# Gathering the first four edge groups straight from the node rows, a table in node order, and a short last group

## The chip, the cores and the metric

The kernel runs on one core of one Trainium2 chip. The metric is the device time of one execution in microseconds (us). The engines are named as in the profile: PE is TensorE (PEld its weight loads), DVE is VectorE, ACT is ScalarE, POOL is GpSimd, SP is SyncE; SPq, POOLq and ACTq are the queues on which these issue DMAs.

## The reference, cut to what matters

```python
x = x + conv(quantise(ln_c(x)), quantise(weight), bias)        # 16 x 64 x 56 x 56
t = tokens(x)                                                  # M = 50176 nodes of 64 channels
h = (ln(t) @ W_gat).reshape(M, 4, 4)                           # 16 features of a node
src, dst = edges + self loops                                  # 262144 edges
a_src, a_dst = (h * att_src).sum(-1), (h * att_dst).sum(-1)    # 4 heads
e = leaky_relu(a_src[src] + a_dst[dst], 0.2)
alpha = exp(e - segment_max(e)) / segment_sum(exp(...))
agg = segment_sum(h[src] * alpha, dst)
scores = layernorm(agg + b_gat).mean over heads                # 4 experts
t = t + sum over the top 2 experts of gate * (gelu(ln(t) @ W1 + b1) @ W2 + b2)
```

The factors exp(a_src - amax) and exp(0.2 (a_src - amax)) depend on the source node only, with amax the maximum over all nodes for each head. They are multiplied on an edge with a factor of its destination.

## The kernel before, in words

There are three stages. In the first, the edges are sorted into 49 blocks of 1024 destination nodes, while the pixels are normalised, quantised and convolved. Its first DVE operations (lines 720 to 733) split the edge list: line 722 takes the block of the destination, lines 725 to 727 turn the source number into a place `(node & 127) * 392 + (node >> 7)`, and lines 728 and 729 code that place in 16 bits. The stage leaves the sorted edges in DRAM (`edge_d`) and one row of 24 floats (96 B) for each node in `node_d`: 16 features, 4 values a_src, 4 values a_dst. The node rows are stored by line 370, two DMAs of 1568 rows for each image.

The second stage is the one that is changed. Edges come as 1090 units of 256 at most (`MAX_UNITS`); 8 units are a group, so there are NG = 137 groups of 16 tiles of 128 edges. The units behind the last real one are padding and read row 0. At the start of the stage:

- SP loads the sorted edges (line 1066), then all node rows into `nodes` with four DMAs (line 1070, 4704 KB in pieces of 96 B).
- DVE decodes the source numbers (line 1329 writes `src_no` and signals `src_ready`), makes the first one-hot masks, waits for the nodes, finds amax (lines 1351 to 1356) and the gaps (lines 1358 to 1360).
- ACT makes `damp` and overwrites the last 8 columns of `nodes` with the two factors (lines 1103 to 1106, `factors_ready`).
- SP then stores the whole table to `tab_d` with one DMA (line 1073), in an order in which each partition writes one contiguous piece (392 rows, 37632 B), and behind it, on the same queue, loads the first tokens `T` (line 1076).
- POOL waits for `src_ready` and `table_stored` (lines 1090 and 1091) and issues one indirect DMA for each tile: 128 rows of 96 B by the numbers in `src_no` (line 1097). `gath` has 4 buffers (`BUFS`) of one group; from group 4 on POOL waits for `rows_used`, which DVE raises in `weigh`.

For each group g, DVE waits for the 16 gathers and weighs the rows (`weigh`, lines 1384 to 1386), spreads them (line 1394, `spread_ready`), and adds up the sums of the group (`add_up`, line 1406) as PE delivers them. PE goes through a fixed order (`body`, line 1255): `up` of the MLP (line 1243, waits for `t_loaded`), half of `scatter` (line 1234, waits for `spread_ready`), transposes of the masks of group g+2 (line 1210), `down` (line 1253), the other half of `scatter`, and `pick_dst` for group g+2 (line 1220, 16 matmuls of 32 columns in two halves). The MLP is part of the bodies of groups 0 to 127; groups 128 to 136 have none. ACT does gelu (line 1120), the bias of the second layer (line 1129), the copies of the turned masks (line 1115) and of the destination factors (line 1142), in an order written out by hand. The first bodies of ACT and PE are unrolled; DVE runs a loop over 33 trips of 4 groups and 5 more groups.

Then the sums are divided and normalised, the gates are made, and the third stage adds the gated experts. Nothing of that is touched.

Of the kernel before, what the change touches and what calls it, by code (L numbers as in the profile page):

```python
# [10 lines left out]
U16 = mybir.dt.uint16  # L11
# [4 lines left out]
P = 128  # L16
# [69 lines left out]
TILES = NG * G  # L86
ID_W = -(-NG * UG // P)
# [52 lines left out]
def build(nc, x, conv_w, conv_b, w_gat, att_src, att_dst, b_gat, ln_g, ln_b, w1, b1, w2, b2, edges, out):  # L140
    ctx = ExitStack()
    with ctx:
# [54 lines left out]
        with ExitStack() as ph:  # L197
# [514 lines left out]
            def _(dve):  # L712
# [12 lines left out]
                L(dve.tensor_scalar(field_i, src[:], LO_BITS, None, ALU.arith_shift_right))  # L725
                L(dve.tensor_scalar(rest_i, src[:], P - 1, None, ALU.bitwise_and))
                L(dve.scalar_tensor_tensor(out=rest_i, in0=rest_i, scalar=float(NQ), in1=field_i, op0=ALU.mult, op1=ALU.add))
                L(dve.tensor_scalar(field_i, rest_i, float(CODE_HALF), float((1 << CODE_SIGN) - CODE_HALF), ALU.is_ge, ALU.mult))
                L(dve.scalar_tensor_tensor(out=rec[:].bitcast(U16)[:, :, 0, :], in0=rest_i.rearrange("p (n t) -> p n t", t=STEP),
# [263 lines left out]
        with ExitStack() as ph:  # L993
            def tb(name, shape, dt=F32):
# [9 lines left out]
            amax = tb("amax", [P, HEADS])  # L1004
            amax_t = tb("amax_t", [HEADS, 1])
# [15 lines left out]
                "nodes_loaded sorted_loaded src_ready pair_added vstep2 amax_rows amax_turned amax_diag amax_spread src_gaps dst_gaps damp_ready factors_ready "  # L1021
# [37 lines left out]
            assert MLP_TRIPS <= TRIPS and UG % 4 == 0 and LAST >= 3  # L1059
# [4 lines left out]
            def _(sp):  # L1064
# [8 lines left out]
                sp.dma_start(tab_d.rearrange("(l q) f -> l (q f)", l=P), nodes[:].rearrange("p q f -> p (q f)")).then_inc(s["table_stored"], 16)  # L1073
# [15 lines left out]
            def _(pool):  # L1089
                pool.wait_ge(s["src_ready"], 1)  # L1090
                pool.wait_ge(s["table_stored"], 16)
                for g in range(NG):
                    if g >= BUFS:
                        pool.wait_ge(s["rows_used"], g - BUFS + 1)
                    for j in range(G):
                        t = g * G + j
                        pool.indirect_dma_start(gath[:, g % BUFS, j, :], None, tab_d,  # L1097
# [3 lines left out]
            def _(act):  # L1101
# [4 lines left out]
                act.activation(nodes[:, :, FEAT + HEADS:ROW], nb[:], ACT.Exp).then_inc(s["factors_ready"], 1)  # L1106

# [66 lines left out]
                stage_dst(2, 2)  # L1174
                for k in range(UNROLL):
                    body(0, k, True)
                with act.Fori(1, MLP_TRIPS) as i:
                    for k in range(UNROLL):
                        body(i, k, True)
# [16 lines left out]
            def _(pe):  # L1196
# [27 lines left out]
                def scatter(g, k, pairs):  # L1224
# [3 lines left out]
                    for w in pairs:  # L1228
# [405 lines left out]
```

## Time and profile before

| | us |
|---|---|
| median of 3 runs | 4512.95 |
| lowest and highest | 4507.73, 4515.62 |
| the profiled execution | 4502.82 |
| its span | 4501.1 |
| POOL busy | 2904.8 (65%) |
| PE busy | 3514.0 (78%) |
| DVE busy | 2830.1 (63%) |
| ACT busy | 1131.1 (25%) |

The span is what the profile shows between the first and the last instruction; the execution's own time is 1.7 us longer. Busy time leaves out DMA issues, except that an indirect DMA on POOL counts as busy while its descriptors are made. Each position below is in us from the start of the span.

### The profile page before, as it was taken

What the parts mean: (1) busy time and instruction counts of PE and PEld (TensorE: products, weight loads), DVE (VectorE), ACT (ScalarE), POOL (GpSimd) and SP (SyncE); (2) the same over time, 40 slices, a digit from 0 to 9 for tenths busy, and PEclk for the clock granted to TensorE, in tenths of its full rate; (3) what the DMA queues carried; (4) which work ended last, traced back from release to release, by engine and by line L of the source; (5) the groups of instructions that cost most, each with busy time, mean ns of one, the idle gap of its engine ahead of it and who ended that gap; (6) DMA issues with size and microseconds to landing.
All of it is one profiled execution on the core that took longest, in us unless ns stands there. A gap on an engine that the chain in (4) does not pass through costs nothing. (4 is left out here: it accounts for less than half of the span.)

```text
span 4501.1 us, 61920 instructions
## 1 busy us (share of the span) xinstructions
PE 3514.0 (78%) x19005; PEld 2450.4 (54%) x19041; DVE 2830.1 (63%) x3531; ACT 1131.1 (25%) x2825; POOL 2904.8 (65%) x2928
## 2 busy tenths in 40 slices
PE   4686332588837999999999999999999999963143
PEld 1454232455525666666666666666666666663011
DVE  7778999888854454554554544545545545445788
ACT  0110000011103333334334333334343343320000
POOL 3000888787735777777777777777777777774055
PEclk8898555688866888989889888889898888876555
DMA  1243111599982222222222222222222222255099
GB/s 50 58 101 82 52 42 52 52 122 116 120 110 66 33 37 33 36 37 33 36 33 37 36 33 36 37 32 37 36 34 36 36 34 36 34 16 6 17 366 332
DMA packets 307960, 284.72 MB, mean 63 GB/s; under 512 B 203555, under 2 KB 280099, under 8 KB 307365
## 3 DMA queue, kind: packets, MB, share of 16 engines
q1 hardware_dynamic: 209556, 202.96, 20.8%
q0 software_dynamic: 87936, 29.35, 9.8%
q10 hardware_dynamic: 10384, 51.39, 5.3%
q8 instruction: 41, 0.67, 0.1%
q14 instruction: 43, 0.34, 0.0%
HBM read 161.21 MB, written 122.27 MB: 63 GB/s over the span
## 5 line engine op out<-in xcount | busy, mean ns | idle before, releaser
L1097 POOL DMA_INDIRECT gath<-tab_d,src_no x2192 | 2068.4, 944 | 752.7 <-issue 667.7
L463 POOL DMA_INDIRECT edge_d<-run_slots,slots x544 | 672.7, 1237 | 579.0 <-ACT run_slots L662 415.7
L1234 PEld LDWEIGHTS C<-spread,lo_hot 128*128 128x128 f32 x4384 | 804.7, 242 | 312.6 <-issue 215.9
L1234 PE MATMUL C<-spread,lo_hot 128*128 128x160 f32 x4384 | 875.9, 367 | 122.7 <-DVE spread L1394 119.5
L1406 DVE TENSOR_TENSOR acc<-acc,C 128x160 f32 x1096 | 351.7, 321 | 914.3 <-PE C L1234 773.1
L1220 PEld LDWEIGHTS C<-dst_rows,lo_hot_t 128*128 128x128 f32 x4384 | 558.6, 207 | 92.1 <-issue 78.3
L1220 PE MATMUL C<-dst_rows,lo_hot_t 128*128 128x32 f32 x4384 | 575.8, 288 | 12.2 <-ACT lo_hot_t L1115 12.2
L1129 ACT ACTIVATE mlp<-A,b2s 64x392 f32<-64x392 f32 x512 | 298.2, 582 | 943.7 <-PE A L1253 943.7
L1243 PE MATMUL A<-T,w1s 64*128 64x392 f32 x1024 | 530.3, 601 | 0.0
L575 PE MATMUL C<-wide_rec,hot_lo 128*128 128x136 f16 x2048 | 272.1, 305 | 299.1 <-DVE wide_rec L840 299.1
L1253 PE MATMUL A<-hid,w2s 128*64 128x392 f32 x1024 | 452.5, 524 | 0.0
L575 PEld LDWEIGHTS C<-wide_rec,hot_lo 128*128 128x128 f16 x2048 | 242.5, 123 | 352.6 <-DVE wide_rec L840 293.1
L1120 ACT ACTIVATE hid<-A,b1s 128x392 f32<-128x392 f32 x512 | 300.9, 588 | 473.8 <-PE A L1243 473.8
L1394 DVE TENSOR_TENSOR spread<-hi_hot,C 128x2560 f32<-128x2560 f32 x137 | 386.4, 2820 | 4.7
L1115 ACT COPY lo_hot_t<-A 128x512 f32<-128x512 f32 x548 | 293.1, 589 | 211.5 <-PE A L1210 211.5
L1210 PEld LDWEIGHTS A<-ident,lo_hot 128*128 128x128 f32 x2192 | 240.5, 142 | 187.4 <-issue 187.2
L1210 PE MATMUL A<-ident,lo_hot 128*128 128x128 f32 x2192 | 302.6, 282 | 36.2 <-PE A L1243 35.6
L1341 DVE TENSOR_TENSOR lo_hot<-C,lo 128x2048 f32<-128x2048 f32 x137 | 314.0, 2292 | 16.6
L1243 PEld LDWEIGHTS A<-T,w1s 64*128 64x128 f32 x1024 | 166.3, 203 | 245.6 <-issue 238.7
L1384 DVE TENSOR_TENSOR C<-gath,C 128x64 f32<-128x64 f32 x137 | 31.4, 229 | 420.8 <-DMA gath<-tab_d,src_no 416.3
L1584 POOL TENSOR_TENSOR four<-pairs 128x392 f32<-128x392 f32 x64 | 64.8, 1013 | 250.8 <-DVE pairs L1605 250.8
L662 ACT CAST run_slots<-C 128x136 f16<-128x136 f32 x32 | 10.0, 312 | 681.8 <-PE C L575 593.0
(268 smaller groups left out, 3266.4 us busy)
## 6 DMA issues: line engine op xcount, KB each, us to landing
mlp_d<-mlp ACTq DMA_DIRECT2D x128, 392.0 KB
mlp<-mlp_d SPq DMA_DIRECT2D x64, 784.0 KB, 6.0
gath<-tab_d,src_no POOLq DMA_INDIRECT x2192
pixels<-in_x SPq DMA_DIRECT2D x32, 392.0 KB, 8.5
src<-in_x SPq DMA_DIRECT2D x32, 392.0 KB, 9.3
T<-t_d SPq DMA_DIRECT2D x128, 98.0 KB
X<-x_d SPq DMA_DIRECT2D x64, 196.0 KB, 7.9
out<-X SPq DMA_DIRECT2D x128, 98.0 KB, 6.6
```

Source lines behind the costliest of these rows:

```text
L463: pool.indirect_dma_start(edge_d, bass.IndirectOffsetOnAxis(ap=slots[:, k, c:c + 1], axis=0), run_slots[:, k, c * RUN:(c + 1) * RUN, :].re ...
L575: mm = pe.matmul(C[:, k, 0:FIELDS * SLOT_COLS], hot_lo[:, j, t // LINE, :, t % LINE], fields[:, t // LINE, :, t % LINE], start=(j == 0 and ...
L1097: pool.indirect_dma_start(gath[:, g % BUFS, j, :], None, tab_d, bass.IndirectOffsetOnAxis(ap=src_no[:, t:t + 1], axis=0)).then_inc(gathere ...
L1120: act.activation(hid[:], A[:, 2, 0:CHUNK], ACT.Gelu, bias=b1s[:, e:e + 1]).then_inc(s["gelu_ready"], 1)
L1210: mm = pe.transpose(A[:, j // 4, (j % 4) * P:(j % 4 + 1) * P], lo_hot[:, k, half * G // 2 + j, :], ident[:])
L1220: mm = pe.matmul(C[:, 0, t * HI * HEADS:(t + 1) * HI * HEADS], lo_hot_t[:, t, :], dst_rows[:, k % 2, t // U].rearrange("p h f -> p (h f)") ...
L1234: mm = pe.matmul(C[:, bank, at:at + HI * VALS], lo_hot[:, k % UNROLL, u * U + j, :], spread[:, u * U + j].rearrange("p h v -> p (h v)"), s ...
L1243: pe.matmul(A[:, 2, 0:CHUNK], w1s[a, e, :], T[a, :], start=True, stop=True).then_inc(s["hidden"], 1)
L1253: pe.matmul(A[h * CH:(h + 1) * CH, 3, 0:CHUNK], w2s[:, e, :], hid[:], start=True, stop=True).then_inc(s["expert_done"], 1)
L1341: dve.tensor_tensor(lo_hot[:, k], lane_v.rearrange("p (k h) -> p k h", k=1).broadcast_to([P, G, P]), lo[:, bass.ds(g * G, G)].rearrange("p ...
L1394: dve.tensor_tensor(spread[:], hi_hot[:, k].rearrange("p t (h k) -> p t h k", k=1).broadcast_to([P, G, HI, VALS]), vals.rearrange("p t (k ...
L1406: L(dve.tensor_tensor(here, here, C[:, bank, at:at + HI * VALS].rearrange("p (h v) -> p h v", h=HI), ALU.add))
```

## The change

The source number is coded as it is (lines 725 to 727 go), and the table is stored in node order by four DMAs in pieces of 96 B. POOL waits for `src_ready` only; the gathers of the first four groups read `node_d`, and the wait for `table_stored` stands before group 4. For groups 0 to 3 ACT makes the two factors on the gathered rows (`raw_factors`), from two small tiles with minus amax; DVE waits for `raw_ready` there. The last group has 2 units (`LAST_UNITS`), so POOL gathers 4 tiles, PE scatters one pair and DVE adds one pair. DVE's first trip of 4 groups is unrolled.

```diff
--- before.py
+++ after.py
@@ -84,6 +84,8 @@
 MAX_UNITS = (EDGES + SG * NB * (RUN - 1) + NB * (U * P - RUN)) // (U * P)
 NG = -(-MAX_UNITS // UG)
 TILES = NG * G
+LAST_UNITS = MAX_UNITS - (NG - 1) * UG
+LAST_TILES = LAST_UNITS * U
 ID_W = -(-NG * UG // P)
 PLACES = NG * UG
 ALL_PLACES = PLACES + SG * RUN_COLS * P // RUN_ROWS
@@ -722,11 +724,8 @@
                 L(dve.tensor_copy(blk_h[:], field_i))
                 by_step = field_i.rearrange("p (n t) -> p n t", t=STEP)
                 rest_i = pos[:].bitcast(I32)
-                L(dve.tensor_scalar(field_i, src[:], LO_BITS, None, ALU.arith_shift_right))
-                L(dve.tensor_scalar(rest_i, src[:], P - 1, None, ALU.bitwise_and))
-                L(dve.scalar_tensor_tensor(out=rest_i, in0=rest_i, scalar=float(NQ), in1=field_i, op0=ALU.mult, op1=ALU.add))
-                L(dve.tensor_scalar(field_i, rest_i, float(CODE_HALF), float((1 << CODE_SIGN) - CODE_HALF), ALU.is_ge, ALU.mult))
-                L(dve.scalar_tensor_tensor(out=rec[:].bitcast(U16)[:, :, 0, :], in0=rest_i.rearrange("p (n t) -> p n t", t=STEP),
+                L(dve.tensor_scalar(field_i, src[:], float(CODE_HALF), float((1 << CODE_SIGN) - CODE_HALF), ALU.is_ge, ALU.mult))
+                L(dve.scalar_tensor_tensor(out=rec[:].bitcast(U16)[:, :, 0, :], in0=src[:].rearrange("p (n t) -> p n t", t=STEP),
                                            scalar=float(CODE_LOW), in1=by_step, op0=ALU.add, op1=ALU.add))
                 L(dve.tensor_scalar(field_i, dst[:], BLK - 1, None, ALU.bitwise_and))
                 L(dve.tensor_scalar(rec[:, :, 1, :], by_step, float(P), None, ALU.add))
@@ -1002,6 +1001,8 @@
             damp = tb("damp", [P, NQ, HEADS])
             blk_row = tb("blk_row", [1, P * ID_W], I32)
             amax = tb("amax", [P, HEADS])
+            fast_gap = tb("fast_gap", [P, HEADS])
+            slow_gap = tb("slow_gap", [P, HEADS])
             amax_t = tb("amax_t", [HEADS, 1])
             amax_d = tb("amax_d", [HEADS, HEADS])
             na = tb("na", [P, NQ, HEADS])
@@ -1018,7 +1019,7 @@
             hid = tb("hid", [P, CHUNK])
             mlp = tb("mlp", [P, EXPERTS, CHUNK])
             s = sems(
-                "nodes_loaded sorted_loaded src_ready pair_added vstep2 amax_rows amax_turned amax_diag amax_spread src_gaps dst_gaps damp_ready factors_ready "
+                "nodes_loaded sorted_loaded src_ready pair_added vstep2 gaps_ready raw_fast raw_ready amax_rows amax_turned amax_diag amax_spread src_gaps dst_gaps damp_ready factors_ready "
                 "table_stored lo_hot_ready dst_rows_ready turned turned_copied picked_ready picked_read rows_used "
                 "spread_ready scattered sp_turns2 act_turns2 "
                 "t_loaded0 t_loaded1 t_used0 t_used1 hidden gelu_ready expert_done expert_out "
@@ -1056,7 +1057,7 @@
             MLP_TRIPS = MLP_CHUNKS * 2 // UNROLL
             TRIPS = (NG - 3) // UNROLL
             LAST = NG - TRIPS * UNROLL
-            assert MLP_TRIPS <= TRIPS and UG % 4 == 0 and LAST >= 3
+            assert LAST_UNITS % 2 == 0 and MLP_TRIPS <= TRIPS and UG % 4 == 0 and LAST >= 3
             raw = lo_hot[:].rearrange("p b t l -> p (b t l)").bitcast(F16)[:, 0:PLACES * RUN * FIELDS]
             RAW_WORDS = PLACES * RUN * FIELDS // 2
 
@@ -1070,7 +1071,9 @@
                     sp.dma_start(nodes[:, k * n:(k + 1) * n, :], node_d.rearrange("(q l) f -> l q f", l=P)[:, k * n:(k + 1) * n, :]).then_inc(s["nodes_loaded"], 16)
 
                 sp.wait_ge(s["factors_ready"], 2)
-                sp.dma_start(tab_d.rearrange("(l q) f -> l (q f)", l=P), nodes[:].rearrange("p q f -> p (q f)")).then_inc(s["table_stored"], 16)
+                for k in range(4):
+                    n = NQ // 4
+                    sp.dma_start(tab_d.rearrange("(q l) f -> l q f", l=P)[:, k * n:(k + 1) * n, :], nodes[:, k * n:(k + 1) * n, :]).then_inc(s["table_stored"], 16)
 
                 for h in range(2):
                     sp.dma_start(T[h * CH:(h + 1) * CH], t_d[0, h * CH:(h + 1) * CH]).then_inc(s[f"t_loaded{h}"], 16)
@@ -1088,13 +1091,14 @@
             @block.gpsimd
             def _(pool):
                 pool.wait_ge(s["src_ready"], 1)
-                pool.wait_ge(s["table_stored"], 16)
                 for g in range(NG):
+                    if g == BUFS:
+                        pool.wait_ge(s["table_stored"], 64)
                     if g >= BUFS:
                         pool.wait_ge(s["rows_used"], g - BUFS + 1)
-                    for j in range(G):
+                    for j in range(G if g < NG - 1 else LAST_TILES):
                         t = g * G + j
-                        pool.indirect_dma_start(gath[:, g % BUFS, j, :], None, tab_d,
+                        pool.indirect_dma_start(gath[:, g % BUFS, j, :], None, node_d if g < BUFS else tab_d,
                                                 bass.IndirectOffsetOnAxis(ap=src_no[:, t:t + 1], axis=0)).then_inc(gathered[g % BUFS], 16)
 
             @block.scalar
@@ -1104,6 +1108,16 @@
                 act.wait_ge(s["src_gaps"], 1)
                 act.activation(nodes[:, :, FEAT:FEAT + HEADS], nb[:], ACT.Exp, scale=0.2).then_inc(s["factors_ready"], 1)
                 act.activation(nodes[:, :, FEAT + HEADS:ROW], nb[:], ACT.Exp).then_inc(s["factors_ready"], 1)
+
+                def raw_factors(g):
+
+                    act.wait_ge(s["gaps_ready"], 1)
+                    act.wait_ge(gathered[g], G * 16)
+                    for h in range(HEADS):
+                        act.activation(gath[:, g, :, FEAT + HEADS + h], gath[:, g, :, FEAT + h], ACT.Exp, bias=fast_gap[:, h:h + 1]).then_inc(s["raw_fast"], 1)
+                    act.wait_ge(s["raw_fast"], (g + 1) * HEADS)
+                    for h in range(HEADS):
+                        act.activation(gath[:, g, :, FEAT + h], gath[:, g, :, FEAT + h], ACT.Exp, bias=slow_gap[:, h:h + 1], scale=0.2).then_inc(s["raw_ready"], 1)
 
                 def turned_copy(g, half):
 
@@ -1172,8 +1186,12 @@
                     for half in range(2):
                         turned_copy(g, half)
                 stage_dst(2, 2)
+                for g in range(2):
+                    raw_factors(g)
                 for k in range(UNROLL):
                     body(0, k, True)
+                    if k + 2 < BUFS:
+                        raw_factors(k + 2)
                 with act.Fori(1, MLP_TRIPS) as i:
                     for k in range(UNROLL):
                         body(i, k, True)
@@ -1226,6 +1244,8 @@
                     if pairs[0] == 0:
                         pe.wait_ge(s["spread_ready"], g + 1)
                     for w in pairs:
+                        if isinstance(g, int) and g == NG - 1 and 2 * w >= LAST_UNITS:
+                            break
                         if w >= 2 or not (isinstance(g, int) and g == 0):
                             pe.wait_ge(s["pair_added"], g * PAIRS + w - 1)
                         for u in range(2 * w, 2 * w + 2):
@@ -1354,6 +1374,8 @@
                 dve.tensor_scalar(amax_d[:], ident[0:HEADS, 0:HEADS], amax_t[:], None, ALU.mult).then_inc(s["amax_diag"], 1)
                 dve.wait_ge(s["amax_spread"], 1)
                 L(dve.tensor_copy(amax[:], A[:, 3, 0:HEADS]))
+                L(dve.tensor_scalar(fast_gap[:], amax[:], -1.0, None, ALU.mult))
+                dve.tensor_scalar(slow_gap[:], amax[:], -0.2, None, ALU.mult).then_inc(s["gaps_ready"], 1)
 
                 L(dve.tensor_tensor(na[:], a_dst, over_nodes(amax[:], HEADS), ALU.add))
                 dve.tensor_scalar(na[:], na[:], 0.0, -0.8, ALU.max, ALU.mult).then_inc(s["dst_gaps"], 1)
@@ -1380,7 +1402,12 @@
                 def weigh(g, i, k):
 
                     weight = vals[:, :, FEAT:VALS]
-                    dve.wait_ge(gathered[k % BUFS], (i * (UNROLL // BUFS) + k // BUFS + 1) * (G * 16))
+                    if isinstance(g, int) and g < BUFS:
+                        dve.wait_ge(s["raw_ready"], (g + 1) * HEADS)
+                    elif isinstance(g, int) and g == NG - 1:
+                        dve.wait_ge(gathered[g % BUFS], g // BUFS * (G * 16) + LAST_TILES * 16)
+                    else:
+                        dve.wait_ge(gathered[k % BUFS], (i * (UNROLL // BUFS) + k // BUFS + 1) * (G * 16))
                     L(dve.tensor_tensor(weight, gath[:, k % BUFS, :, FEAT:FEAT + HEADS], dst_damp, ALU.mult))
                     L(dve.tensor_tensor(weight, gath[:, k % BUFS, :, FEAT + HEADS:ROW], weight, ALU.max))
                     dve.tensor_tensor(vals[:, :, 0:FEAT].rearrange("p t (h d) -> p t h d", h=HEADS),
@@ -1398,7 +1425,7 @@
                 def add_up(g):
 
                     qs = unit_blocks(dve, g)
-                    for u in range(UG):
+                    for u in range(LAST_UNITS if isinstance(g, int) and g == NG - 1 else UG):
                         bank, at = bank_of(u)
                         if u % 2 == 0:
                             dve.wait_ge(s["scattered"], g * PAIRS + u // 2 + 1)
@@ -1422,7 +1449,9 @@
                 pick_damp(0, 0)
                 weigh(0, 0, 0)
                 spread_out(0, 0)
-                with rolled(dve, 0, TRIPS, step, UNROLL * (4 + UG)) as i:
+                for k in range(UNROLL):
+                    body(0, k)
+                with rolled(dve, 1, TRIPS, step, UNROLL * (4 + UG)) as i:
                     for k in range(UNROLL):
                         body(i, k)
                 for k in range(LAST):
```

## Rows read from the trace of the kernel before

**Rows 1.** POOL's gathers: count, duration ns, first and last start, and what its idle time ended on.
```profile
L1097 POOL DMA_INDIRECT gath<-tab_d,src_no x2192: 940/944/985, 1376.3 to 4111.5; - x200
  issue: 667.7, 2191
  DMA tab_d<-nodes: 85.0, 1
```

**Rows 2.** The page's costliest groups: the weighing on DVE (busy, mean ns | idle before, releaser).
```profile
L1384 DVE TENSOR_TENSOR C<-gath,C 128x64 f32<-128x64 f32 x137 | 31.4, 229 | 420.8 <-DMA gath<-tab_d,src_no 416.3
```

**Rows 3.** Timeline of the start of stage two: start us, us, engine, line, instruction.
```profile
1299.69 36.65 SPq L1070 DMA_DIRECT2D nodes<-node_d  x4
...
1319.50 1.30 DVE L1329 TENSOR_SCALAR src_no<-spread 128x2192 int32<-128x2192 int32 x1
...
1347.64 4.07 DVE L1351 TENSOR_REDUCE amax<-nodes 128x4 f32<-128x1568 f32 x1 [13.65 <-DMA nodes<-node_d]
...
1360.93 1.99 ACT L1142 COPY dst_rows<-damp 128x32 f32 x16
1361.05 0.36 SPq L1073 DMA_DIRECT2D tab_d<-nodes  x1
...
1384.48 1.28 ACT L1120 ACT_TABLE_LOAD   x1
...
1387.13 1.67 PE L1243 MATMUL A<-T,w1s 64*128 64x392 f32 x2
```

**Rows 4.** Timeline of the first groups.
```profile
1397.50 0.23 DVE L1384 TENSOR_TENSOR C<-gath,C 128x64 f32<-128x64 f32 x1 [21.87 <-DMA gath<-tab_d,src_no]
...
1401.36 4.63 PE L1234 MATMUL C<-spread,lo_hot 128*128 128x160 f32 x16 [12.56 <-DVE spread L1394]
...
1417.70 0.23 DVE L1384 TENSOR_TENSOR C<-gath,C 128x64 f32<-128x64 f32 x1 [3.34 <-DMA gath<-tab_d,src_no]
...
1456.25 0.94 POOL L1097 DMA_INDIRECT gath<-tab_d,src_no  x1 [0.30 <-issue]
```

**Rows 5.** Windows: PE, PEld, DVE, ACT, POOL busy; then PEclk, DMA share, GB/s.
```profile
1320.00:1330.00 10.00, 0.00 (x0) 0.00 (x0) 9.72 (x9) 0.00 (x0) 0.00 (x0) 0.50 1.33 131
1400.00:1405.00 5.00, 3.64 (x14) 3.64 (x15) 4.84 (x5) 0.00 (x0) 3.79 (x4) 0.50 0.14 10
4050.00:4070.00 20.00, 11.09 (x79) 10.74 (x78) 9.94 (x16) 3.20 (x12) 15.12 (x17) 0.74 0.88 10
```

**Rows 6.** The stores of the node rows and of the table (lines 370 and 1073).
```profile
DMA to landing us min/median/max: 3.0/9.9/12.2
...
DMA to landing us min/median/max: 14.4/14.4/14.4
```

**Rows 7.** TensorE in a stretch of long and then short groups (timeline, and one window).
```profile
2235.77 1.42 PE L1220 MATMUL C<-dst_rows,lo_hot_t 128*128 128x32 f32 x12
...
2300.00:2310.00 10.00, 10.00 (x39) 7.36 (x38) 5.17 (x9) 2.71 (x11) 7.56 (x8) 0.66 0.30 50
...
2421.26 0.98 PE L1220 MATMUL C<-dst_rows,lo_hot_t 128*128 128x32 f32 x8
...
2473.36 0.86 PE L1220 MATMUL C<-dst_rows,lo_hot_t 128*128 128x32 f32 x7
```

**Rows 8.** The last group on DVE.
```profile
4119.61 0.23 DVE L1384 TENSOR_TENSOR C<-gath,C 128x64 f32<-128x64 f32 x1 [8.27 <-DMA gath<-tab_d,src_no]
...
4126.12 0.79 DVE L1406 TENSOR_TENSOR acc<-acc,C 128x160 f32 x2 [2.70 <-PE C L1234]
...
4130.56 0.78 DVE L1406 TENSOR_TENSOR acc<-acc,C 128x160 f32 x2 [0.52 <-PE C L1234]
```

**Rows 9.** DVE at the start of the program.
```profile
11.72 1.23 DVE L725 TENSOR_SCALAR run<-src 128x2048 int32<-128x2048 int32 x1
...
16.57 2.35 DVE L728 TENSOR_SCALAR run<-pos 128x2048 int32<-128x2048 int32 x1
```

## The prediction

> **What bounds the kernel now.** I read the page first and then the line with the largest sum of busy and idle time, POOL's gathers. There are 2192 of them from 1376.3 to 4111.5, and all their idle time but one wait is issue [rows 1]. So POOL never waits once it has begun: (4111.5 - 1376.3) / 2191 = 1.248 us a gather, 19.97 us a group of 16. The one wait is 85.0 us at the start, for the table. DVE is idle 416 us for gathers before it weighs [rows 2], so the consumers are mostly faster than POOL. The stage therefore lasts as long as POOL's chain. It can get shorter by an earlier start of that chain, by fewer gathers, or by a shorter path behind the last one. Before trusting this I looked whether PE would be next, since it is nearly always busy: in one stretch nine groups in a row took PE (2421.26 - 2235.77) / 9 = 20.61 us each, more than POOL's 19.97, and the three after them (2473.36 - 2421.26) / 3 = 17.37 [rows 7]. In the long groups the granted clock is at its lower level (1.2 GHz) for a part of each group (mean 0.66 in a window of 10 us with PE busy throughout), in the short ones not. PE had not stood still before these drops; what it had run last was the 32-column matmuls. This matters for a rival below.
>
> **Three operations at the start.** Lines 725 to 727 go; the next one starts at 16.57 where line 725 started at 11.72 [rows 9], so 4.85 us go. DVE then feeds the masks, the ranks and the sort; nothing there waits for something that isn't moved with it. I take all 4.85 us; the ends are 0 and 4.85.
>
> **POOL's start.** It now waits for `src_no` only, written at 1319.50 + 1.30 = 1320.8 [rows 3]. That is 55.5 us before 1376.3. (From here on positions are those of the trace, without the 4.85.) The first 64 gathers take 64 x 1.248 = 79.9 us, so POOL would be at group 4 at 1400.7, where the trace has 1456.25 [rows 4]. Two things can hold it there.
>
> First, the table. The nodes land a little later, because gathers run beside the load: a gather stream has a DMA share of 0.14 where the node load has 1.33 [rows 5], so I take 10% of the 27 us that overlap, 2.8 us. DVE has two more operations on 4 columns ahead of the gaps, 0.4 us together at the most (a larger one takes 0.23 [rows 4]). The factors are ready at 1361.0 + 2.8 + 0.4 = 1364.2 instead of 1361.0 [rows 3]. The old store landed in 14.4 us [rows 6]; the new one has pieces of 96 B, 50176 of them. No such store stands in the trace, the nearest is the node load, its mirror image: 131 GB/s [rows 5], so 4.82 MB take 36.8 us. With 1.8 us of latency (gather 31 ends at 1376.3 + 31 x 1.248 + 0.9 = 1415.9, DVE goes on at 1417.70 [rows 4]) and 10% of 38.6 for the gathers beside it, it lands at 1364.2 + 38.6 + 3.9 = 1406.7. Bounds: not below the 14.4 us of the large pieces, which ends before 1400.7 and means no wait at all; above, line 370 lands 2 x 1568 rows of 96 B in 3.0 us at best [rows 6], 16 times that is 48 us, with 10% 53 us, landing at 1417. Its median of 9.9 us is not scaled up: those stores stood in the queue behind whole images. I take 1406.7, so group 4 starts 49.5 us earlier than before (ends 55.5 and 39).
>
> Against this stands a rule of the Trainium skill ("DMA: Bandwidth & Descriptors", Specifications): below 512 B an engine does a read-modify-write. If that doubled the 36.8 us, the table would land at 1364.2 + 73.6 + 1.8 + 7.5 = 1447 and POOL would gain 9 us rather than 49.5; the 3.0 us of line 370 speak against a doubling.
>
> Second, `rows_used`. Group 4 needs the weighing of group 0. ACT's `raw_factors` stand behind the turned copies, about where it loads the gelu table at 1384.48 [rows 3], 3 us later now. They are 8 exps on 16 columns a group; 16 small copies took 1.99 us [rows 3], so 1 us a group, bounds 0.5 and 3. DVE weighs group 0 at about 1389, before 1397.50, and in time for POOL. Groups 2 and 3 cost ACT four table loads of 1.28 us in all [rows 3] and 2 us of exps, while PE does the scatter; bounded at 7 us once, if nothing hid them.
>
> **What is late next: T.** SP issues `T` behind the table, on the same queue. The four node DMAs kept SP for 36.65 us [rows 3], so `T` is issued near 1400 and lands about 2 us behind the table, at 1409. PE's first `up` ran at 1387.13 [rows 3] and stands in front of the first scatter, so that scatter moves from 1401.36 [rows 4] to 1410.5, and the second weighing, free at 1417.70 - 3.34 = 1414.4 before, to 1423.5. The chain of PE and DVE is thus 9 us later than before, while POOL is 49.5 us ahead. POOL may be ahead by four buffers: it is held when a group is weighed more than 79.9 - 21.4 - 0.9 = 57.6 us behind its landing. Group 4 lands at 1406.7 + 21.6 = 1428.3 and is weighed at 1423.5 + 3 x 17.4 or 20.6 = 1476 to 1485, so 47 to 57 us behind. That is just inside; I take 2 us of hold. Afterwards the distance shrinks if PE's mean is under 19.97: nine long and three short groups [rows 7] make (9 x 20.61 + 3 x 17.37) / 12 = 19.8, and the short ones ended only where PE had caught up. From group 128 on there is no MLP and DVE idles some 8 us of each group [rows 8], so nine groups make up for nearly 60 us whatever is left. POOL's chain ends 49.5 - 2 = 47.5 us earlier.
>
> **The last group.** POOL leaves 12 gathers out, 15.0 us. But DVE was ready for the last weighing at 4119.61 - 8.27 = 4111.3 [rows 8], still busy with the group before, so 8.3 us are gained. Then one pair is added instead of four: it ends at 4126.91 rather than at 4131.34 [rows 8], 4.4 us. Together 12.7 us; ends 8 and 17. The gathers of this end are slow in landing (they all read row 0, DMA share 0.88 at the 10 GB/s of the others [rows 5]), yet with 4 of them they have 10 us more than they need.
>
> **Sum.** 4.85 + 47.5 + 12.7 = 65 us. On the profiled execution, 4502.8 us, that gives 4438; on the median of the runs, 10 us higher, 4448. I forecast the median, 4448.
>
> **Rivals.**
> 1. The table lands before POOL is there and nothing holds it: 4.85 + 55.5 + 12.7 = 73 us, 4440. The large-piece store speaks for it, the node load against. 0.15.
> 2. Small writes at twice the price of small reads (73.6 us, landing at 1364.2 + 73.6 + 1.8 + 7.5 = 1447): 4.85 + 9 + 12.7 = 27 us, 4486. 0.12.
> 3. The early gathers don't run at 1.248 us beside a saturated node load (share 1.33). If those until 1350 were held back, group 4 would start at 1350 + 80 = 1430: 26 us instead of 49.5, 4470. Against it: in the padding the share is 0.88 and POOL keeps its pace (15.12 busy of 20 [rows 5]). 0.10.
> 4. Slower than before: PE becomes the bound. It starts 9 us late; if it had the long group every time, group 128 would be weighed at 1423.5 + 127 x 20.61 = 4041 and could land no earlier than 57.6 us before that, 3983, where it landed at 1376.3 + 128 x 19.97 + 18.7 + 2.7 = 3954 before. 29 us later, less 12.7 and 4.85: 11 us slower, 4524. It costs from a mean of 20.0 us a group on and turns the sign at 20.5. The nine long groups speak for it, the three short ones against. 0.05.
> 5. The stage is moved, but something outside the sum gives it back, no difference: 0.03.
>
> **How the numbers follow.** The forecast has 0.55. A measurement of this kernel can't tell less than about 0.2% (9 us) from no change. All cases but 4 and 5 are faster by more: 0.92; 0.03 same; 0.05 slower. The range goes from a little under case 1 (tail at its end, 4436) to just short of case 2, 4482.
>
> **What would show it.** POOL's first gather at about 1316 (1320.8 less 4.85), before amax is there; the wait for `table_stored` at group 4 a few us long, and then only issue again; the node load 3 us longer; four issues of the table on SP of some 9 us each; the first `up` waiting for `T`; the weighings about 50 us behind their gathers at first and DVE without waits for gathers for some tens of groups, then waits again; the last weighing right behind the add of group 135. It is wrong if POOL waits for the table over 15 us, if POOL waits for `rows_used` again and again in the middle, or if gathers in the first 60 us are longer than 1.25 us apart.

## The result and the profile after

The changed kernel takes 4451.49 us (median of 4 runs, 4446.86 to 4457.73) where the kernel before took 4514.28 beside it (4 runs, 4507.73 to 4520.28): ratio 0.9859, 95% interval [0.9846, 0.9873], so 62.8 us less. Forecast were 4448 and a gain of 65 us. The profiled execution took 4457.73 us with a span of 4456.0, 6.2 us above its median; that of before was 11.5 us below its own. So the two traces differ by 45.1 us only, and what they show in single terms has to be read against that.

These are lines of the page after, the costliest groups (instructions, busy us, mean ns of one | idle before and its releaser). The first answers to the page's line behind [rows 1]: 2116 gathers with the line of the table, and 64 others with the node rows. TensorE's wait for `T` is new.

```profile
L1101 POOL DMA_INDIRECT gath<-tab_d,src_no x2116 | 2001.5, 946 | 645.2 <-issue 645.2
L465 POOL DMA_INDIRECT edge_d<-run_slots,slots x544 | 676.5, 1244 | 577.2 <-ACT run_slots L664 413.9
...
L1263 PE MATMUL A<-T,w1s 64*128 64x392 f32 x1024 | 529.9, 601 | 22.0 <-DMA T<-t_d 22.0
```

The answer for the line of the gathers, as [rows 1] (duration ns min/median/max, first and last start; then what its idle time ended on, and who waited for it). POOL starts with the source numbers and waits for nothing else in the whole stage: neither the table nor `rows_used` has a line. But the longest of the 64 node-row gathers took 2519 ns.

```profile
L1101 POOL DMA_INDIRECT gath<-tab_d,src_no x2116: 942/947/962, 1414.8 to 4060.2; - x193
L1101 POOL DMA_INDIRECT gath<-node_d,src_no x64: 942/947/2519, 1323.3 to 1413.5; - x64
its engine sat idle before it (us, times) until:
  issue: 664.4, 2179
  DVE src_no L1349: 29.8, 1
who waited for it (us, times):
  DVE C L1411: 163.3, 49
```

DVE waits 163.3 us in all for gathers, where it was 416.3 [rows 2]: up to group 74 it is now DVE that is behind, and POOL that runs ahead.

POOL reaches group 4 at 1414.76, 91.4 us after its start, where 79.9 were expected. Eleven of the 64 gathers are longer than the others. The timeline of the first gathers beside DVE (start us, us, engine, line, instruction, idle before) shows the first part of the missing 11.5 us: the first three take 2.4 to 2.5 us each, and the fourth, when DVE has turned to operations that read `C`, a PSUM tensor (L1359, L1361), takes 0.94.

```profile
1323.09 2.63 DVE L1352 CAST spread<-lo_hot 64x2192 int32<-64x2192 f16 x2
1323.32 2.52 POOL L1101 DMA_INDIRECT gath<-node_d,src_no  x1 [29.82 <-DVE src_no L1349]
...
1326.15 2.36 POOL L1101 DMA_INDIRECT gath<-node_d,src_no  x1 [0.30 <-issue]
...
1328.81 2.37 POOL L1101 DMA_INDIRECT gath<-node_d,src_no  x1 [0.30 <-issue]
...
1331.43 2.29 DVE L1361 TENSOR_TENSOR lo_hot<-C,lo 128x2048 f32<-128x2048 f32 x1
1331.49 0.94 POOL L1101 DMA_INDIRECT gath<-node_d,src_no  x1 [0.30 <-issue]
```

From there to 1357.76 all gathers are short, beside the saturated node load (DMA share 1.36 from 1340 to 1350) and beside DVE's reduction. Eight more are long, from 1359.01 to 1376.67, each beside DVE's work on the node columns; the two that start while DVE waits for ACT (1363.51, 1364.76) are short.

```profile
1351.66 4.07 DVE L1371 TENSOR_REDUCE amax<-nodes 128x4 f32<-128x1568 f32 x1 [15.42 <-DMA nodes<-node_d]
1352.75 0.96 POOL L1101 DMA_INDIRECT gath<-node_d,src_no  x1 [0.31 <-issue]
...
1357.89 1.78 DVE L1380 TENSOR_TENSOR na<-nodes,amax 128x1568 f32<-128x1568 f32 x1
1359.01 1.79 POOL L1101 DMA_INDIRECT gath<-node_d,src_no  x1 [0.30 <-issue]
...
1363.51 0.95 POOL L1101 DMA_INDIRECT gath<-node_d,src_no  x1 [0.30 <-issue]
...
1365.44 1.79 DVE L1386 TENSOR_TENSOR nb<-nodes,damp 128x1568 f32<-128x1568 f32 x1 [3.06 <-ACT nodes L1110]
1366.01 2.05 POOL L1101 DMA_INDIRECT gath<-node_d,src_no  x1 [0.31 <-issue]
...
1370.10 7.27 DVE L1390 TENSOR_TENSOR acc<-nodes,nb 128x1568 f32<-128x1568 f32 x4
1370.49 2.22 POOL L1101 DMA_INDIRECT gath<-node_d,src_no  x1 [0.30 <-issue]
...
1378.50 0.94 POOL L1101 DMA_INDIRECT gath<-node_d,src_no  x1 [0.30 <-issue]
```

The start of the groups, as [rows 3, 4]: the table's four DMAs hold SP from 1365.36 to 1399.36, ACT does its exps early (two times 4 in 0.99 us a group), DVE weighs group 0 at 1391.01, and `T` keeps TensorE until 1413.54, with the scatter and the first add behind it.

```profile
1365.36 11.86 SPq L1076 DMA_DIRECT2D tab_d<-nodes  x2
...
1388.89 0.99 ACT L1117 ACTIVATE gath<-gath,fast_gap 128x16 f32<-128x16 f32 x4
...
1391.01 0.23 DVE L1411 TENSOR_TENSOR C<-gath,C 128x64 f32<-128x64 f32 x1 [11.07 <-ACT gath L1120]
...
1399.40 11.74 SPq L1079 DMA_DIRECT2D T<-t_d  x2
1413.54 1.67 PE L1263 MATMUL A<-T,w1s 64*128 64x392 f32 x2 [22.04 <-DMA T<-t_d]
1415.14 3.30 PE L1254 MATMUL C<-spread,lo_hot 128*128 128x160 f32 x11
...
1417.79 0.32 DVE L1433 TENSOR_TENSOR acc<-acc,C 128x160 f32 x1 [19.12 <-PE C L1254]
```

From there DVE is behind POOL and weighs without a wait, until its first wait for gathers at 2856.81, at group 75. At the end it weighs group 136 (4074.55) with no wait, right behind the last pair of group 135, where [rows 8] have 8.27 us of wait, and adds one pair.

```profile
4073.62 0.78 DVE L1433 TENSOR_TENSOR acc<-acc,C 128x160 f32 x2 [0.30 <-PE C L1254]
4074.55 0.23 DVE L1411 TENSOR_TENSOR C<-gath,C 128x64 f32<-128x64 f32 x1
...
4081.90 0.32 DVE L1433 TENSOR_TENSOR acc<-acc,C 128x160 f32 x1 [0.52 <-DVE acc L1433]
```

How the 45.1 us of the two traces add up: group 4 starts 41.5 us earlier (1414.76 against 1456.25). The last gather starts at 4060.2 against 4111.5; of these 51.3 us, 15.0 are 12 gathers left out, so the chain itself has 36.3 left. The 5 us between are the pace: (4060.2 - 1414.8) / 2115 = 1.2508 us a gather in this trace, 1.2484 in that of before. Four experiments below (table_wait2, one_store, t_first2, combo) ran at 1.2482 to 1.2483, so it isn't the change's. The last add ends at 4082.22 against 4131.34, 49.1 us earlier, and the later stages take 4 us more in this trace.

### The profile page after: what moved, and what is told of

It reads as the page before. It is cut to its first block and busy times, and to the rows that moved or that the text cites. A ratio compares the mean times of both kernels' runs of the same rounds, so it can differ in the third digit from the quotient of the medians.

```text
span 4456.0 us, 61803 instructions
## 1 busy us (share of the span) xinstructions
PE 3488.1 (78%) x18981; PEld 2429.2 (55%) x19017; DVE 2828.8 (63%) x3524; ACT 1145.3 (26%) x2861; POOL 2913.9 (65%) x2916
## 5 line engine op out<-in xcount | busy, mean ns | idle before, releaser
L1101 POOL DMA_INDIRECT gath<-tab_d,src_no x2116 | 2001.5, 946 | 645.2 <-issue 645.2
L465 POOL DMA_INDIRECT edge_d<-run_slots,slots x544 | 676.5, 1244 | 577.2 <-ACT run_slots L664 413.9
L1254 PEld LDWEIGHTS C<-spread,lo_hot 128*128 128x128 f32 x4360 | 785.1, 238 | 261.2 <-issue 196.0
L1254 PE MATMUL C<-spread,lo_hot 128*128 128x160 f32 x4360 | 856.0, 363 | 73.3 <-DVE spread L1421 68.9
L1361 DVE TENSOR_TENSOR lo_hot<-C,lo 128x2048 f32<-128x2048 f32 x137 | 314.0, 2292 | 16.1
L1156 ACT COPY dst_rows<-damp 128x32 f32 x1096 | 144.7, 215 | 76.4 <-issue 60.4
```

What stands on the lines that cost most here:

```text
L465: pool.indirect_dma_start(edge_d, bass.IndirectOffsetOnAxis(ap=slots[:, k, c:c + 1], axis=0), run_slots[:, k, c * RUN:(c + 1) * RUN, :].re ...
L1101: pool.indirect_dma_start(gath[:, g % BUFS, j, :], None, node_d if g < BUFS else tab_d, bass.IndirectOffsetOnAxis(ap=src_no[:, t:t + 1], a ...
L1254: mm = pe.matmul(C[:, bank, at:at + HI * VALS], lo_hot[:, k % UNROLL, u * U + j, :], spread[:, u * U + j].rearrange("p h v -> p (h v)"), s ...
L1361: dve.tensor_tensor(lo_hot[:, k], lane_v.rearrange("p (k h) -> p k h", k=1).broadcast_to([P, G, P]), lo[:, bass.ds(g * G, G)].rearrange("p ...
```

## The experiments

Some of the experiments ran on chips where every kernel, that of before too, took some 6400 us, with a mean granted clock of 0.68 to 0.69; each ratio below is to runs of the kernel before on the same chip. Positions are compared from the issue of the edge load, with which stage two begins (1300.0 in the trace of the changed kernel, 1297.8 in that of before).

My theory was the forecast's: the stage is POOL's chain, and the time follows its start, its length and the path behind it. Rivals were that the changed store costs something by itself, that `T` behind it does, and that DMA traffic lengthens the gathers.

**All of the old wait, with the new table.** POOL waits for the table before its first gather.

```diff
                 pool.wait_ge(s["src_ready"], 1)
+                pool.wait_ge(s["table_stored"], 64)
                 for g in range(NG):
-                    if g == BUFS:
-                        pool.wait_ge(s["table_stored"], 64)
```

> The changed kernel, but POOL waits for the whole table before its first gather (the first four groups still read the node rows and get their factors from ACT). No gather runs beside the node load or the store, so this shows what the store in 96 B pieces takes by itself. Theory (a write of 96 B costs what a read costs): the store lands 38.6 us after the factors, POOL starts 24 us later than in the kernel before, and the time is 24 - 12.7 - 5 = 6 us over the kernel before (4520). Rival (small writes cost twice): it lands 75 us after the factors, 43 us over (4557). If the early start were not what brought the gain, this kernel would stay near the changed one (4451).

On a 6400 us chip it came out at 1.0023 [1.0003, 1.0043]. It was run again on one of the usual chips.

> The kernel of table_wait again, POOL waits for the whole table before its first gather. Theory (a write of 96 B costs what a read costs): POOL starts some 39 us after the factors are ready, at about 1401 on the scale of the trace before, 24 us later than there; time 6 to 11 us over the kernel before (ratio 1.001 to 1.003). Rival (small writes at twice the price): 43 us over (1.0095). If the early start were not what brings the gain: 0.986.

Ratio 1.0025 [1.0011, 1.0038]: 4516.83 against 4501.94. The store with its 96 B pieces is issued at 1374.07 and POOL goes on at 1421.72, so it takes 47.6 us with no gather beside it. Here is the answer for its gathers:

```profile
L1100 POOL DMA_INDIRECT gath<-node_d,src_no x64: 940/944/990, 1421.7 to 1500.4; - x64
its engine sat idle before it (us, times) until:
  issue: 664.0, 2179
  DMA tab_d<-nodes: 117.2, 1
```

The same 64 gathers of node rows, now behind DVE's long operations, take 1501.7 - 1421.7 = 80.0 us, and none is over 0.99 us. Against the changed kernel group 4 starts 86.9 us later, 76.5 from the start of the stage; the ratios differ by 0.0166, 75 us, give or take 9 by their intervals. So within that the time follows POOL's start one for one, and the early gathers are the whole of the gain at the start: with the new store and the old wait the kernel is 11 us slower than before, short last group and all. In the store's time the core moved 102 to 111 GB/s, here one of the windows (as [rows 5]), where the node load has 131:

```profile
1390.00:1400.00 10.00, 8.79 (x40) 8.40 (x40) 0.00 (x0) 2.01 (x10) 0.00 (x0) 0.50 1.52 111
```

**The old store.** The table is written in one DMA with large pieces, in the old order; from group 4 on the gathers then fetch the rows of other nodes, as many and as large.

```diff
-                for k in range(4):
-                    n = NQ // 4
-                    sp.dma_start(tab_d.rearrange("(q l) f -> l q f", l=P)[:, k * n:(k + 1) * n, :], nodes[:, k * n:(k + 1) * n, :]).then_inc(s["table_stored"], 16)
+                sp.dma_start(tab_d.rearrange("(l q) f -> l (q f)", l=P), nodes[:].rearrange("p q f -> p (q f)")).then_inc(s["table_stored"], 16)
...
-                        pool.wait_ge(s["table_stored"], 64)
+                        pool.wait_ge(s["table_stored"], 16)
```

> The changed kernel, but the table is stored by one DMA in the order of before (so the rows gathered from group 4 on belong to other nodes; the values are wrong, the work is the same). The store lands in some 15 us instead of under 45, and T right behind it. In the changed kernel POOL was never held by the table, but eight of its first 64 gathers took 1.5 to 2.2 us around 1359 to 1377, beside the start of the store. Theory: those long gathers come from the four small-row stores being issued; with one store they go, POOL is 5 to 7 us ahead at group 4, and the time is 5 us less (4446). Rival a: they come from the store's traffic as such, which the single store makes denser: no difference. Rival b: the small rows cost more than that: 10 us or more.

Ratio 0.9865 [0.9848, 0.9881], no difference to 0.9859. The store is issued at 1351.61 and takes 15.0 us. Two of the long gathers start before it, at 1345.08 and 1347.36, where the DMA share (window 1340 to 1350) is 0.09. The answer for the gathers:

```profile
L1099 POOL DMA_INDIRECT gath<-tab_d,src_no x2116: 940/944/961, 1400.9 to 4041.0; - x193
L1099 POOL DMA_INDIRECT gath<-node_d,src_no x64: 940/944/2517, 1309.4 to 1399.7; - x64
```

The 64 gathers take 91.5 us, with the same 11 long ones. So my theory was wrong: the long gathers come neither from the four stores being issued nor from their traffic. The small-piece store costs nothing here, since POOL comes later than it lands.

**T ahead of the table.** The first load of `T` moves in front of SP's wait for the factors.

```diff
+                for h in range(2):
+                    sp.dma_start(T[h * CH:(h + 1) * CH], t_d[0, h * CH:(h + 1) * CH]).then_inc(s[f"t_loaded{h}"], 16)
                 sp.wait_ge(s["factors_ready"], 2)
...
-                for h in range(2):
-                    sp.dma_start(T[h * CH:(h + 1) * CH], t_d[0, h * CH:(h + 1) * CH]).then_inc(s[f"t_loaded{h}"], 16)
```

> The changed kernel, but SP loads T ahead of the table. PE's first up no longer waits 22 us and the chain of PE and DVE starts about 20 us earlier. Theory: POOL's chain alone sets the end, PE had caught up with it by group 75; so no difference (4451, within 3 us), only the catching up ends earlier, by some 25 groups. Rival: the start of the PE chain counts, 10 to 22 us faster (4430 to 4441).

0.991 [0.9878, 0.9941] on a 6400 us chip. In its answer for the gathers POOL waits for DVE in 132 of the 137 groups, so there the consumers set the time and the question wasn't put.

```profile
its engine sat idle before it (us, times) until:
  DVE C L1413: 1883.5, 132
```

On a usual chip:

> The kernel of t_first again, SP loads T ahead of the table. In t_first every kernel, the one before too, took over 6300 us and POOL waited for the consumers in every group, so it said nothing on a POOL that never waits. Theory: the chain of PE and DVE starts some 20 us earlier, catches up with POOL earlier, and the time stays that of the changed kernel (ratio to before 0.986, within 0.001). Rival: the consumers' start counts, 10 to 22 us faster (0.981 to 0.984).

Ratio 0.9856 [0.9839, 0.9872], again no difference, and the interval leaves nearly nothing of the rival's 0.981 to 0.984. The timeline of DVE has the first add at 1403.23, with the edge load at 1303.1; that is 17.7 us earlier in the stage than the 1417.79 of the changed kernel, with its 1300.0.

```profile
1403.23 0.79 DVE L1433 TENSOR_TENSOR acc<-acc,C 128x160 f32 x2 [1.04 <-PE C L1254]
```

An earlier consumer is worth nothing while POOL is not held.

**T later still.** Four more stores of the node rows to a spare place ahead of `T`.

```diff
+                for k in range(4):
+                    n = NQ // 4
+                    sp.dma_start(spare_d.rearrange("(q l) f -> l q f", l=P)[:, k * n:(k + 1) * n, :], nodes[:, k * n:(k + 1) * n, :]).then_inc(s["spare_stored"], 16)
                 for h in range(2):
                     sp.dma_start(T[h * CH:(h + 1) * CH], t_d[0, h * CH:(h + 1) * CH]).then_inc(s[f"t_loaded{h}"], 16)
+                sp.wait_ge(s["spare_stored"], 64)
```

The declarations of the spare tensor and of its semaphore are not shown.

> The changed kernel with the table stored a second time, to a spare tensor, ahead of T. PE's first up waits some 47 us longer. In the changed kernel the weighing was up to 55.7 us behind the landing of its group, and POOL is held where that passes 57.6 us. Theory: the four buffers are used up at once, POOL is held about 40 us around group 5 and a few us more until the first short groups, and all of it stays in the time: about 43 us more than the changed kernel, ratio 0.995. Rival: the consumers make up for it, since PE catches up on its own: no difference (0.986).

> The kernel of t_late again (the table stored a second time, to a spare tensor, ahead of T), for a chip on which POOL never waits in the changed kernel. Theory: PE's first up comes some 45 us later than in the changed kernel, POOL is held about 40 us at groups 5 to 9 because the four buffers are full, and nothing gives it back: about 43 us more than the changed kernel, ratio 0.995. Rival: PE catches up and nothing is lost, 0.986.

Both ran on 6400 us chips only: 0.9922 [0.9894, 0.995] and 0.9928 [0.9904, 0.9952]. In the second the first `up` waits for `T` for 65.5 us, until 1517.86, instead of 21.8 in the trace of the long last group on such a chip (long_last2), and yet the ratio is that of the kernels without it there (0.991 with `T` first, 0.9919 with the long last group, below). My limit of 57.6 us for the distance between a gather's landing and its weighing would have called for a loss. But on these chips POOL waits for the consumers in 132 groups anyway, so the limit was not tested; it stays argued.

**The last group.** Once the changed kernel with the long last group, and once the kernel before with the short one.

```diff
-LAST_UNITS = MAX_UNITS - (NG - 1) * UG
+LAST_UNITS = UG
```

The kernel before gets the lines of the change that make its last group short.

> The changed kernel, but the last group has its full 8 units again (16 gathers, 4 pairs). Theory: the end of stage two is POOL's last gather plus a path behind it, of which the short group takes 8.3 us of waiting and 4.4 us of adding. So this is 12.7 us slower than the changed kernel (about 4464 where that had 4451). Rival a: the 12 gathers count in full, 15.0 us for POOL plus 4.4 for the adds, 19 us (4471). Rival b: DVE is so far behind POOL that the last group is hidden, 0 to 4 us. The last weighing should again wait some 8 us for gathers in the first case.

> The kernel of long_last again (last group with all 8 units), for a POOL that never waits. Theory: 12.7 us slower than the changed kernel, ratio to before 0.9887; in the trace some 8 us of waiting before the last weighing, and 39.8 us from the last gather of group 135 to the end of the adds, as before, where the changed kernel has 27. Rival a (gathers count in full): 19 us, 0.990. Rival b (hidden): 0 to 4 us, 0.986.

> The kernel before with the short last group alone. The same 12.7 us, now as a gain: about 4502 against 4514. Rival a says 19 us (4495). It also has the stage one of before, with the three operations, so its first stage should end some 5 us later than those of the kernels built from the changed one, if those operations lie on the path.

All three met 6400 us chips: 0.9939 [0.9918, 0.9959], 0.9919 [0.9895, 0.9943] and 0.9984 [0.9963, 1.0006]. They show nothing on the 12.7 us. The first two had no run of the changed kernel on their chip beside them, the interval of the third holds 1, and the groups there are some 34 us apart instead of 20. What the last group brings on a usual chip rests on the two traces (below), not on an experiment.

**What lengthens the gathers, and a faster version.** If it is DVE's work on SBUF, leaving that work out must shorten them. First a version that tries to gain more: node loads wait for the edges, DVE decodes the source numbers of the first 5 groups ahead of the rest, 5 groups come from node rows, and `T` is first.

```diff
+RAW = 5
...
+                sp.wait_ge(s["sorted_loaded"], 16 * (PARTS_U + 1))
...
-                    if g == BUFS:
+                    if g == RAW:
+                        pool.wait_ge(s["src_ready"], 2)
...
+                decode(0, RAW * G)
...
+                decode(RAW * G, TILES)
```

> The changed kernel with four more steps: SP waits for the sorted edges before it issues the node load (the edges land sooner), DVE decodes the source numbers of the first five groups ahead of the others (9.4 us of decoding become about 2), five groups instead of four are gathered from the node rows, and T is loaded ahead of the table. POOL's first gather should be 8 to 13 us earlier than in the changed kernel after the same stage one, group 5 should not wait for the table, and PE's chain starts 20 us earlier. Theory (POOL's chain sets the end): 8 to 13 us faster than the changed kernel, 4440 where that had 4451, ratio to the kernel before 0.983. Rival a: the node load is pushed back and POOL waits for the table at group 5 for as much as it gained: no difference to the changed kernel (0.986). Rival b: the consumers' start counts as well: 20 to 30 us faster (0.980).

Ratio 0.9828 [0.9811, 0.9844]: 4430.36 against 4507.68, the lowest of all ratios. In its answer no wait holds POOL once it has begun:

```profile
L1104 POOL DMA_INDIRECT gath<-node_d,src_no x80: 940/944/2716, 1312.1 to 1427.2; - x80
its engine sat idle before it (us, times) until:
  issue: 663.4, 2177
  DVE src_no L1354: 21.4, 1
  DVE C L1421: 0.3, 1
  DMA tab_d<-nodes: 0.3, 1
```

The first gather comes 14.8 us after the edge load's issue (at 1297.25) instead of 23.3, 8.5 us earlier. But it now starts among more of DVE's decoding, and 15 gathers are long instead of 11: the 80 take 1428.4 - 1312.1 = 116.3 us instead of 99.9. At group 5 it is 131.2 us into the stage, the changed kernel 1414.8 + 20.0 - 1300.0 = 134.8. So 3.6 us of the 14 us between the ratios (0.0031) are seen in the chain. For the rest I have no cause; the intervals of the two ratios leave some 10 us to either side of the 14.

Then the same with DVE's seven operations that begin the sums (the self loops) replaced by a memset, so that the self loops are missing from the sums:

```diff
-                L(dve.tensor_tensor(nb[:], slow, damp[:], ALU.mult))
...
+                L(dve.memset(acc[:], 1.0))
```

> The kernel of combo, but DVE leaves out the seven operations that put the self loops into acc and fills acc with a constant instead (the self loops are missing from the sums). In every trace a gather on POOL takes 0.95 us while DVE is idle or reads PSUM, and 1.5 to 2.7 us while DVE works on SBUF alone; eight of the long ones lie beside these seven operations and the gaps. Theory: DVE's SBUF work slows the making of the descriptors, so the gathers beside the seven operations get short, group 5 starts about 6 us earlier after the first gather (110 us where combo has 116.3) and the time is 6 us less than combo's (ratio 0.9815 where combo had 0.9828). Rival: the DMA traffic of the store makes them long; then they stay long, 116 us.

It ran on a 6400 us chip (0.987 [0.985, 0.9891]), but what it was made for is in its timeline:

```profile
1405.26 1.78 DVE L1388 TENSOR_TENSOR na<-nodes,amax 128x1568 f32<-128x1568 f32 x1
...
1406.10 2.06 POOL L1104 DMA_INDIRECT gath<-node_d,src_no  x1 [0.30 <-issue]
...
1408.47 2.10 POOL L1104 DMA_INDIRECT gath<-node_d,src_no  x1 [0.30 <-issue]
...
1414.47 6.59 DVE L1394 MEMSET acc<- 128x7840 f32 x1 [4.71 <-issue]
1414.62 0.94 POOL L1104 DMA_INDIRECT gath<-node_d,src_no  x1 [0.30 <-issue]
```

The seven long gathers beside DVE's decoding are there as in combo. Behind them only the two beside the operations on the node columns that stayed are long, and the six beside the seven that went are short again, beside the same table store: the first 64 gathers start within 89.5 us instead of 95.1, 5.6 us less, where about 6 were expected. That is the cause shown for these six: DVE's operations on SBUF lengthen the gathers that POOL issues beside them; the store's transfers don't, and neither does a memset. For the long ones beside the decoding no operation was taken out; there the cause rests on the timelines, in which they end when DVE turns to operations that read PSUM, with the node load still running.

## Why the prediction was right

**The mechanism held.** The stage is POOL's chain. The trace has no wait in it behind the first one, and taking the early start away gave back 75 us of ratio for 76.5 us of start. Two parts of the path to group 4 were not as forecast, the pace of the first gathers and the wait for the table.

**POOL's start.** Predicted 55.5 us earlier, 1320.8 less 4.85. It is 23.3 us into the stage where `src_no` was written 23.0 us into that of before: right.

**The first 64 gathers at 1.248 us** were the step that failed: 91.4 us instead of 79.9. It is one of the prediction's own signs of being wrong, gathers in the first 60 us more than 1.25 us apart, and it came. Rival 3 had gathers that don't run at their pace, held back by the load's traffic for 24 us; the size is half of that and the cause another one. The trace of before could have told it. Its page has this line of the other indirect DMAs, in stage one:

```profile
L463 POOL DMA_INDIRECT edge_d<-run_slots,slots x544 | 672.7, 1237 | 579.0 <-ACT run_slots L662 415.7
```

They take 1237 ns in the mean, and the shortest takes 952. In the changed kernel's trace the same line (L465) runs from 956 to 3097 ns. A mean so far above the least is a sign that something holds the engine up, and the gathers were about to be moved to a time in which DVE works on SBUF.

**The table.** Predicted 38.6 us and 3.9 for gathers beside it, measured 47.6 without any: close to the upper bound, which scaled line 370's 3.0 us. The node load was a poor mirror image, by a factor 1.2. The Trainium skill ("DMA: Bandwidth & Descriptors", Specifications) says that below 512 B an engine does a read-modify-write. Whether that is what happens no run shows, but the doubling of rival 2, 75.4 us with the latency, did not come. What was measured, less 1.8 us of latency, is 45.8 us or 1.24 times the 36.8 us of the load's rate, as the 102 to 111 GB/s against 131 have it too. The wait for the table at group 4, forecast at 6 us (1400.7 to 1406.7), did not come. That the slower store cost nothing is luck, since two errors of the same sign hid each other: by its 47.6 us the table landed at about 1365.4 + 47.6 = 1413.0, and POOL, itself 11.5 us late, arrived for it at 1414.76. Had the gathers run at 1.248, POOL would have stood there from 1403.2 and gained some 2 us only. The old store moved nothing because the long gathers were there.

**The hold by `rows_used`**, 2 us, didn't come. The distance between a group's landing and its weighing, put at 47 to 57 us, was 51 to 55.7 for groups 1 to 9, just under the limit of 57.6. From there to group 75 it shrank, since the weighings were 19.2 us apart in the mean: they came in eights, four over 20.5 us and four under 19.1 (20.52, 20.61, 20.71, 20.63, 17.27, 17.37, 17.45, 19.04). The 19.8 from nine long and three short groups was on the safe side, and rival 4, which begins to cost at 20.0, did not come.

**ACT's exps** took 1.98 us a group instead of 1, inside 0.5 to 3, and are hidden. **T** landed for 1413.54; forecast were 1409, 1411 with this trace's later stage.

**The last group.** From the start of the last gather of group 135 to the end of the adds it takes 27.0 us, before 39.8: 12.8 us, where 12.7 were worked out.

**The three operations.** The same DVE instructions start 4.3 to 4.9 us earlier up to 171 us; by 206 us that is lost. From 170 to 200 us the granted clock is 0.85, 0.50 and 0.97 in three stretches of 10 us where the trace of before has 1.00, 0.83 and 1.00. The start of stage two lies between 1286.5 and 1310.4 in five traces with the same stage one, that of before at 1297.8, so 4.85 us can be neither confirmed nor denied there. This term of the sum stays open, and was not tried alone.

**The sum.** From the traces: 43.7 us for the chain's start (41.5 and the 2.2 us by which this trace's stage begins later), 12.8 for the end, makes 56.5, and with 4.85, if it is real, 61.4. Measured are 62.8 on the medians, 57 to 70 by the interval. The forecast of 65 is 3.6 us above the 61.4, since its term for the chain was 47.5 instead of 43.7. That it came within 2.2 us of the medians is closer than its terms deserve.

## What to carry to other kernels

When a chain of DMA issues on GpSimd is moved to an earlier time, look at what VectorE does in that time: put the issues beside work with PSUM operands or reductions, or take the slower pace, up to 3.0 us from one issue to the next instead of 1.25 in these traces, into the sum. A consumer that is behind by nearly all the buffers cost nothing here, as long as its mean was shorter than the producer's, and an earlier consumer gained nothing. For a chain that never waits, the time follows its start one for one, so the first thing to look for is data that is ready earlier, even in a form that costs extra work elsewhere.

## What the runs showed of the hardware

- An indirect gather of 128 rows takes POOL 0.94 to 0.96 us, and 1.4 to 2.7 us while VectorE runs certain operations on SBUF: f32 tensor-tensor operations with both inputs there (1.78 us for 1568 columns), and casts, copies and tensor-scalars at about twice that rate (0.98 us for 1568, 1.30 for 2192). Beside a reduction of one SBUF input (4.07 us), a memset (6.59 us) and operations with an operand in PSUM it keeps its 0.94 to 0.96. The Trainium skill ("GPSIMD Engine Reference", Key points) says that GpSimd shares its SBUF interfaces with VectorE and contends with instructions in a 2-port mode or with two SBUF inputs; the traces agree with that, if the operations at twice the rate are those in a 2-port mode, which a trace doesn't name, and they add the price: 11 long gathers made 11.5 us.
- A store of 50176 pieces of 96 B took 47.6 us at 102 to 111 GB/s, the same 4.8 MB in large pieces 15.0 us, and the load of the same pieces ran at 131 GB/s.
- The chips on which the kernels took 1.42 times as long are not explained. POOL's gathers kept their 0.94 us there. In the trace of t_late2 DVE's adds stood still 1528 us in all (148 times, at most 14.2) on something that the trace only calls remote.
